# A decoder layer on one core: the last attention's output projection and norm moved into the first middle stage, other steps moved up at the seams

## The reference

```python
x = _layernorm(x + retention(x))          # q, k, v, gate; 16 heads; group norm per head; gate * ret @ wo + bo
x = _layernorm(x + ssm(ctx, gate_by=x))   # conv of 4 taps, silu, selective scan of 16 states, y * silu(x)
x = _layernorm(x + moe(x))                # 8 experts as low-rank additions to one FFN of 896, top 2
# ssm, with dt = softplus(dt_proj(dt_lo)):
state = state * exp(dt * A) + (dt * u) * B ;  y = sum_n state * C + D * u
# moe, for each of the two chosen experts e with routing weight rw:
x1 = x @ W1.T + lora1_e(x);  x3 = x @ W3.T + lora3_e(x);  h = silu(x1) * x3
out += (h @ W2.T + lora2_e(h)) * rw
```

## Time and profile before

| | |
|---|---|
| runs (us) | 480.14, 480.17, 482.71; median 480.17 |
| the profiled execution: its time, its span | 480.21, 478.5 |
| TensorE busy, VectorE, ScalarE, GpSimd | 391.9 (82%), 301.8 (63%), 189.8 (40%), 191.3 (40%) |
| mean granted TensorE clock | 0.913 of 2.4 GHz |

### The profile page before, as it was taken

How to read it: one execution, slowest core, us unless ns; L and a number is a source line. 1 busy time by engine, 2 the same in 40 slices (tenths; PEclk the granted TensorE clock), 3 DMA queues, 4 the chain that set the end, 5 groups by cost and what they waited for, 6 DMA issues and landing times.

```text
span 478.5 us, 7162 instructions
## 1 busy us (share of the span) xinstructions
PE 391.9 (82%) x2552; PEld 335.2 (70%) x2552; DVE 301.8 (63%) x643; ACT 189.8 (40%) x462; POOL 191.3 (40%) x207
## 2 busy tenths in 40 slices
PE   3776986878778557989798788979977899999993
PEld 2454765667556446889587778958776898789992
DVE  5546465675884619999236899942779993382224
ACT  3681557444424614453423635432264532131010
POOL 6015455246320454772214677131377632141221
PEclk9957899989859568999979899997989999999999
DMA  7640270000002101230300133020003300000000
GB/s 223 230 179 18 78 242 1 23 22 2 13 24 88 40 6 44 90 121 0 92 0 24 44 111 103 10 90 2 22 34 115 96 23 0 0 2 23 1 1 22
DMA packets 12339, 27.03 MB, mean 56 GB/s; under 512 B 1800, under 2 KB 3088, under 8 KB 12048
## 3 DMA queue, kind: packets, MB, share of 16 engines
q1 hardware_dynamic: 11440, 25.00, 15.8%
q10 hardware_dynamic: 864, 1.57, 1.0%
HBM read 25.39 MB, written 1.18 MB: 56 GB/s over the span
## 4 chain that ended last, share of the span: by engine, by line
PE 42%; DVE 30%; issue 14%; ACT 5%; POOL 5%; DMA 1%; SPq 1%; DVEq 0%; POOLq 0%; ACTq 0%
PE gen L1051 12%; PE xf L1051 11%; PE a2p L1051 9%; DVE ret L1597 6%; PE ret L1051 6%; DVE gen L1597 6%; DVE fth L1858 3%; PE acc L1051 3%; DVE ring L1605 2%; DVE sc L1614 2%; DVE ring L1671 2%; DVE cv L1537 2%; DMA wattn_sb<-in_wattn 1%; PE xf L1130 1%; POOL rs L598 1%
## 5 line engine op out<-in xcount | busy, mean ns | idle before, releaser
L1051 PE MATMUL xf<-am,wsplit 128*128 128x256 f32 x672 | 97.3, 296 | 0.1
L1051 PEld LDWEIGHTS xf<-am,wsplit 128*128 128x128 f32 x672 | 88.3, 197 | 2.2 <-DVE work L1869 0.5
L567 POOL TENSOR_TENSOR ring<-decay,brow 128x512 f32<-128x512 f32 x48 | 62.1, 1307 | 21.4 <-PE acc L1051 20.3
L672 POOL TENSOR_TENSOR work<-work,ratioT 128x256 f32<-128x256 f32 x28 | 20.6, 737 | 110.7 <-DVE work L1869 110.5
L1858 DVE SCALAR_TENSOR_TENSOR fth<-fth,xf 128x256 f32<-128x256 f32 x56 | 23.3, 415 | 62.2 <-ACT fth L998 62.1
L1051 PE MATMUL a2p<-work,wff_sb 128*128 128x256 f32 x224 | 60.1, 392 | 0.5 <-POOL work L672 0.5
L998 ACT ACTIVATE fth<-xf 128x256 f32<-128x256 f32 x56 | 20.9, 374 | 83.7 <-PE xf L1051 78.4
L1051 PE MATMUL xf<-x2s,wsplit 128*128 128x256 f32 x336 | 51.2, 303 | 0.4
L1051 PE MATMUL acc<-ident,ring 128*128 128x128 f32 x256 | 38.9, 281 | 12.8 <-DVE ring L1605 12.5
L1051 PEld LDWEIGHTS xf<-x2s,wsplit 128*128 128x128 f32 x336 | 45.4, 198 | 2.1 <-DVE work L1869 1.1
L1051 PEld LDWEIGHTS acc<-ident,ring 128*128 128x128 f32 x256 | 31.1, 145 | 18.6 <-DVE ring L1605 14.9
(11 more groups left out here) (278 smaller groups left out, 752.9 us busy)
## 6 DMA issues: line engine op xcount, KB each, us to landing
brow<-bc_dram SPq DMA_DIRECT2D x24, 256.0 KB, 3.6
crow<-bc_dram SPq DMA_DIRECT2D x24, 256.0 KB, 3.2
work<-in_wsp SPq DMA_DIRECT2D x3, 896.0 KB, 9.1
wff_sb<-in_wff SPq DMA_DIRECT2D x2, 896.0 KB, 7.7
am<-bc_dram SPq DMA_DIRECT2D x1, 1536.0 KB, 7.7
wattn_sb<-in_wattn SPq DMA_DIRECT2D x1, 1280.0 KB, 5.7
xT_sb<-in_xT SPq DMA_DIRECT2D x4, 256.0 KB, 2.7
wff_sb<-in_wff SPq DMA_DIRECT2D x3, 256.0 KB, 4.8
```

The source lines that it names most:

```text
L567: pool.tensor_tensor(ring[:, i % RING], du_of(b)[:, j].unsqueeze(1).broadcast_to([P, UN, S]), brow[:, c % 2], ALU.mult).then_inc(sem["driv ...
L672: pool.tensor_tensor(xs[:, n % 4], fq[:, m % 2], ratioT[:], ALU.mult).then_inc(sem["xs_ready"], 1)
L1051: return pe.matmul(o, l, r, skip_group_check=True, **kw)
```

## The change

The slots of `first` go from 21 to 18. The last attention's projection is in n = 2 of the first middle stage, its add and statistics in n = 3, root, shift and apply in n = 4. In `first`, GpSimd's `inputs` and two drives go from slot 16 to 15, `bias(3)` to 17, `start_y` on ScalarE from slot 17 to 16; GpSimd's `mk1` add goes behind the two lows. The finished batch's norm is applied by ScalarE (`finished`), behind a shift by VectorE (`norm_shift` for `norm_apply`), and ScalarE issues all stores.

In the stages: on TensorE `start_y` goes from n = 0 to 1, `base(12)` ahead of `flip_x2`, `low_rank` behind `logits`, `down` 2 and 3 to n = 12, 4 to n = 13, 5 behind it; A1 comes in n = 12; `route_rows` and `step_size` come ahead of `shrink(12)`, MK and MD ahead of `shrink(13)` and A3 behind MD. On VectorE the conv's first two steps go from n = 9 to the start of n = 11, the other four to its end, `conv_gate` from n = 10 to the start of n = 13, between the two parts of `route`, `second_part` to the start of n = 12. On ScalarE `normed`, `turned` and `rounded` are at the end of n = 11, `conv_tanh`, `weighed` and `low_rank` in n = 12, `routed`, softplus and its logarithm after n = 13 and ahead of `spread`, `start_y` ahead of the second pair of `am_high`, the decays behind it. DBL and DT are in bank 1.

```diff
...
-    a2_ready=3, down_done=1, r3_ready=8, r3_pow=1, y_ready=2,
+    a2_ready=3, down_done=1, r3_ready=8, r3_pow=1, y_shift=1, y_ready=2,
 )
...
 -SLOTS = 21
+SLOTS = 18
...
 ROTATED = gen_order()
-STAGED = []
+STAGED = [("OUT", B - 1)]
 for _b in range(1, B):
     _n = [_b + 1] if _b + 1 < B else []
-    STAGED += [("Z", _b)] + [("IN", n) for n in _n] + [("DBL", n) for n in _n] + [("X2", _b)] + [("DT", n) for n in _n]
-    STAGED += [(name, _b) for name in ("LG", "A1", "A3", "RT", "MK", "MD", "RW")]
+    STAGED += [("Z", _b)] + [("IN", n) for n in _n] + [("X2", _b), ("LG", _b)] + [("DBL", n) for n in _n] + [("A1", _b), ("RT", _b)]
+    STAGED += [("DT", n) for n in _n] + [(name, _b) for name in ("MK", "MD", "A3", "RW")]
...
-OWN_BANK = {("X2", 0): 4, ("A1", 0): 5, ("A3", 0): 2, ("VAR", B - 1): 0, ("RW", 0): 0, ("OUT", B - 1): 0}
+OWN_BANK = {("X2", 0): 4, ("A1", 0): 5, ("A3", 0): 2, ("VAR", B - 1): 0, ("RW", 0): 0}
...
-GEN_AT += [{"X2": 1, "A1": 5, "A3": 1}.get(name, 0) for name, _ in STAGED]
+GEN_AT += [{"X2": 1, "DBL": 1, "DT": 1, "A1": 5, "A3": 1}.get(name, 0) for name, _ in STAGED]
...
-DOWNS = {10: (0, 1), 11: (2,), 12: (3, 4), 13: (5,)}
+DOWNS = {10: (0, 1), 12: (2, 3)}
...
-            def store(fb):
-                need(sp, "y_ready", fb, 2)
-                sp.dma_start(of(out, fb), yo[:]).then_inc(sem["y_out"], 16)
...
                 spread(b)
-            store(B - 1)
             need(sp, "y_out", B, 0)
...
                 mkT = mkTs[b % 2]
-                pool.tensor_tensor(mkT[:, 1], mkT[:, 0], mkT[:, 1], ALU.add).then_inc(sem["mk1_ready"], 1)
                 for i in (2, 3):
...
                                        ).then_inc(sem["aml_pool"], 1)
+                pool.tensor_tensor(mkT[:, 1], mkT[:, 0], mkT[:, 1], ALU.add).then_inc(sem["mk1_ready"], 1)
...
                         root(b, ve, rs, "r2_ready", 9, "r2_pow")
-                    if i == 16:
+                    if i == 15:
                         inputs(nb)
...
                         drive_unit(nb, 1)
+                    if i == 16:
+                        second_masks(b)
+                    if i == 17:
                         bias(B - 1)
-                        second_masks(b)
...
                         root(fb - 1, ve3, rs3, "r3_ready", 8, "r3_pow")
+                    if n == 4 and fb == 0:
+                        root(B - 1, ve1, rs1, "r1_ready", 7, "r1_pow")
                     if b is not None:
...
                         decays(nb, 0)
+                        start_y(nb)
                     if i == 17:
-                        start_y(nb)
                         decays(nb, 1)
...
+            def finished(fb):
+                need(act, "y_shift", fb, 1)
+                for t in range(NT):
+                    act.activation(yo[:, t], r3[:, t], ACT.Identity, bias=nm3[:, t:t + 1], scale=rs3[:, t:t + 1]
+                                   ).then_inc(sem["y_ready"], 1)
+                need(act, "y_ready", fb, 2)
+                act.dma_start(of(out, fb), yo[:]).then_inc(sem["y_out"], 16)
             def stage(b, fb, nb):
                 for n in range(len(MAIN)):
-                    if b is not None and n == 11:
-                        normed(b)
                     need(act, "xf_filled", fb, n + 1)
...
                     if n == 2 and fb > 0:
-                        need(act, "y_ready", fb - 1, 2)
-                        act.dma_start(of(out, fb - 1), yo[:]).then_inc(sem["y_out"], 16)
+                        finished(fb - 1)
+                    if n == 4 and fb == 0:
+                        attended(B - 1)
                     if n == 4:
...
                         act.activation(keep[:], x2[:], ACT.Copy).then_inc(sem["keep_ready"], 1)
-                    if nb is not None:
-                        if n == 8:
-                            conv_input(nb)
-                        if n == 10:
-                            conv_tanh(nb)
-                        if n == 11:
-                            low_rank(nb)
-                    if b is not None and n == 12:
+                    if nb is not None and n == 8:
+                        conv_input(nb)
+                    if b is not None and n == 11:
+                        normed(b)
                         turned(b)
...
                     if nb is not None and n == 12:
-                        softplus_exp(nb)
-                    if b is not None and n == 13:
+                        conv_tanh(nb)
+                    if b is not None and n == 12:
                         weighed(b)
+                    if nb is not None and n == 12:
+                        low_rank(nb)
+                if b is not None:
+                    routed(b)
                 if nb is not None:
+                    softplus_exp(nb)
                     softplus_log(nb)
                 if b is not None:
-                    routed(b)
                     spread(b)
...
                 if nb is not None:
-                    decays(nb, 0)
+                    start_y(nb)
                 if b is not None:
...
                 if nb is not None:
-                    start_y(nb)
+                    decays(nb, 0)
                     decays(nb, 1)
...
                     ratios(b)
+                if b is None:
+                    finished(fb)
...
                         shrink(fb, n - LAG)
-                    hidden(fb, n, n <= 1)
+                    hidden(fb, n, n <= 1 or n == 12 and b is not None)
+                    if n == len(MAIN) - 1 and b is not None:
+                        route_rows(b)
+                        if nb is not None:
+                            step_size(nb)
+                        down(fb, 4)
                     if n >= LAG:
...
                     if b is not None:
-                        if n == 0:
+                        if n == 1:
                             start_y(b, fb)
...
                             add_states(b, i)
+                        if n == 2 and fb == 0:
+                            attention_out(B - 1)
                         if n == 4:
                             token_z(b)
-                    if nb is not None:
-                        if n == 7:
-                            context(nb)
-                        if n == 11:
-                            low_rank(nb)
+                    if nb is not None and n == 7:
+                        context(nb)
                     if b is not None and n == 11:
+                        base(fb, 12)
                         flip_x2(b)
-                    if nb is not None and n == 12:
-                        step_size(nb)
                     if b is not None and n == 12:
                         logits(b)
+                        if nb is not None:
+                            low_rank(nb)
                     for m in sums.get(n, ()):
                         down(fb, m)
-                    if b is not None and n == 13:
+                    if b is not None and n == 12:
                         expert_inputs(b, "A1", A1)
-                        expert_inputs(b, "A3", A3)
                 if b is not None:
-                    route_rows(b)
+                    spread_rows(b, "MK", 0)
+                    down(fb, 5)
+                    spread_rows(b, "MD", 1)
+                    expert_inputs(b, "A3", A3)
                 shrink(fb, len(MAIN) - 1)
...
                     base(b, 1)
-                    spread_rows(b, "MK", 0)
-                    spread_rows(b, "MD", 1)
                 down(fb, FM - 1)
...
-            def conv(b):
+            def conv(b, i0=0, i1=2 * DC - 2):
...
                         i = 2 * k + j
+                        if not i0 <= i < i1:
+                            continue
                         if i >= 2:
...
                 dve.scalar_tensor_tensor(nm_[:], mv_[:, :, 0], -1.0, rs_[:], ALU.mult, ALU.mult).then_inc(sem[done], 1)
-            def norm_apply(b, src, mv_, rs_, dst, pow_, done):
-                need(dve, pow_, b, 1)
-                for t in range(NT):
-                    dve.tensor_scalar(dst[:, t], src[:, t], mv_[:, t, 0:1], rs_[:, t:t + 1], ALU.subtract, ALU.mult
-                                      ).then_inc(sem[done], 1)
...
                     units = SCANS[n] if b is not None else []
+                    if nb is not None and n == 11:
+                        conv(nb, 0, 2)
                     if b is not None and n == 11:
                         norm_shift(b, mv, rs, nm, "r2_pow", "r2_shift")
+                    if b is not None and n == 12:
+                        second_part(b)
+                    if b is not None and n == 13:
+                        route(b, 0)
+                        if nb is not None:
+                            conv_gate(nb)
+                        route(b, 1)
                     for i in units[:1]:
...
                     if n == 2 and fb > 0:
-                        norm_apply(fb - 1, r3, mv3, rs3, yo, "r3_pow", "y_ready")
```

(22 more changed lines are left out.)

## The result

The changed kernel takes 457.12 us (median of 4 runs, 456.57 to 457.71) against 480.15 us of the kernel before in the same comparison: ratio 0.9509, 95% interval 0.9474 to 0.9545. The forecast was 455.0, its own range 450 to 460. The profiled execution took 456.57 us with a span of 454.8, 23.7 us less than before, at a mean clock of 0.928 (0.913 before).

A forecast was written before the change was run, and what follows sets the result against it. VectorE was taken to bound the scan stretches and TensorE the seams, with a 9.05 us hole ending `first`. Terms 9.0 + 2.0 - 0.5 + 12.0 + 2.5 = 25.0 us gave 455.0 us, range 450 to 460.

The forecast's parts named there:

- first hole: End of `first`, where TensorE idles 9.05 us waiting for `gated(3)`: moving the last attention gains 9.0 us net.
- seams one and two: Passages between stages with a next batch: reordered products and banks gain 6.0 us each, 12.0 us.
- norm: Finished batch's norm leaves VectorE in the scan stretch of two stages: 1.0 us each, 2.0 us gained.
- seam three: The seam with no next batch: only the `base(12)`, `shrink(11)` and `down` moves, 2.5 us gained.
- tail: End of the kernel, where nothing covers the norm's shift and ScalarE's apply: 0.5 us lost.
- signs set for being right: Timeline marks: first tanh near 169.6, second stage's scan 1 14 to 17 us earlier, 2 to 3 us gap before MD.
- signs of being wrong: Seam stretch at clock 0.50 over 4 us, VectorE idle over 2 us among scans, first stage's start waiting for GpSimd.
- TensorE's balance: Seam lower bound of 1.8 us: 4.3 us idle and 1.95 us lost to the clock before, 4.4 us idle after.
- The seams give nothing: Rival, chance 0.17: seams one and two's new waits and a clock fall after each take all their gain, 467.2 us.
- The first hole does not close: Rival, chance 0.05: a late bank or buffer release leaves scan 1 gaining 3 us instead of 12.2, 464.2 us.
- Slower: Rival, chance 0.05: TensorE stays at 1.2 GHz from `low_rank`'s wait to next stage's n = 2, both seams, 493 us.
- Everything fits: Rival, chance 0.12: no clock fall, 7.9 us gained at two seams and 3.5 at the third, 450.4 us.

The follow-up runs named there:

- e1: The kernel before with only the last attention's move (slots 21 to 18, its steps into n = 2 to 4): 470.61 us, ratio 0.9792.
- e4: The changed kernel with GpSimd's `inputs` and two drives of `first` back in slot 16: 455.98 us, ratio 0.9499.
- e9: The changed kernel with `inputs` and drives of `first` back in slot 16 and `low_rank` behind `down` 2 and 3: 451.15 us, ratio 0.9372.
- e3: The changed kernel with the finished batch's norm applied by VectorE again, as before the change: 461.15 us, ratio 0.9587.
- e6: The changed kernel with `low_rank` behind `down` 2 and 3 in n = 12 instead of ahead of them: 454.68 us, ratio 0.9441.
- e8: The changed kernel with the edits of e4, e6 and e7 together: 452.28 us, ratio 0.9388.
- e2: The changed kernel without the last attention's move (21 slots again), so seams, norm and slot moves only: 463.87 us, ratio 0.9658.
- e10: e8 plus a wait: at a seam GpSimd's two drives start only when VectorE has written both lows: 448.46 us, ratio 0.9311.
- e7: The changed kernel with MK copied ahead of the softplus logarithm and mask slot 0 ahead of `step_sum`: 459.07 us, ratio 0.9514.
- e5: The changed kernel unaltered, run again for comparison on one chip: 457.97 us, ratio 0.9518.

## Why the prediction was right, and which term was off

The measured span is 23.7 us shorter for a forecast of 25.0. The parts are further off than the sum, and partly cancel: first hole 2.3 us too much, seams one and two 1.6 too little, norm and seam three 0.4 too much each, tail 0.2 too little. Three of the signs set for being right did not come: the first tanh is at 172.74 (169.6), scan 1 of the second stage 13.5 us earlier (14 to 17), the gap before MD 1.19 us (2 to 3). The others did. Of the signs of being wrong, a start that waits for GpSimd came in a hidden form: ScalarE waits for VectorE, which GpSimd's drives had held up.

**First hole** (taken 9.0 us: 12.2 at the first tanh less 3.2; measured 6.7: 9.0 at the first tanh and 9.4 at scan 1, less 2.7 from there to the last scan). This is the mis-sized term. The mechanism holds: no wait for `gated(3)`, the attention's steps between the scans (add at 187.41, between scans 5 and 6), 0.84 us lost behind the apply at n = 4 for a forecast of 1.0. The step that failed is that GpSimd's `inputs` and drives in slot 15 were costed by their own durations (2.50 us) alone, as a move on GpSimd's queue. Beside VectorE's lows they took 3.34, the lows 2.36 instead of 1.29, the shift 1.21 instead of 0.15, and so VectorE's `gvar` and the last two masked products behind it came 2.1 us late.

ScalarE's `am_high` waits for these products: at 164.77, after 4.24 us idle, where it stood at 161.63 after 2.10 us before. Everything of ScalarE up to the first tanh is queued behind it, the decay of scan 0 too; `norm_lin`, at 170.53, waits for nothing of its own. The forecast said of ScalarE's inputs that they hold; this one did not.

e1, e4 and e9 show it: with the drives in slot 16, e9's lows start at 160.01, as the changed kernel's at 159.97, and its scan 0 at 167.73 instead of 169.83. The forecast had the drives end near 161.5; they end at 163.45. The remaining 1 us of the tanh is where this execution stood already when the last part of `first` began: a product of the router's rows that both profiles have is at 151.42, 150.41 before, and 150.3 to 153.0 over the experiments. What makes this part differ is not shown.

The long shift of 1.21 us had a row and was made a bound, for the moved shifts. There it proved rightly short (0.15 and 0.16 us). Whether GpSimd's drives would lengthen the large lows as well, which the moved drives now met, was not asked, nor whether they would lengthen L1916 in the seams.

**The norm** (2.0): 0.8 us in each of two stages, 1.6. The apply of 1.08 us is covered by the scans, as argued; e3 gives 1.9 for it. **The tail** (-0.5): -0.3.

**Seams one and two** (6.0 each): 6.8 each. The forecast lay between 7.9 without and 5.5 with a fall of the clock. In the profiled execution the clock did not fall, so the working's own value was 7.9, and the gain was 1.1 short of it. The last masked input ends at 248.37, 5.9 us earlier beyond the first hole's 6.7, for a forecast of 7.0; some 0.75 of the missing 1.1 us are L1916's (1.44 us for 0.69), between `shrink(13)` and the lows on that path.

The clock was misread. The forecast counted 3.9 us at a granted clock of 0.50 before the change and 1.95 us lost. That was the length of the stretch chosen; the rows beside it have 0.96 and 0.95, and the clock was at 0.50 from 238.3 to 245.1, for 6.8 us, which costs 3.4. TensorE's balance then gives a lower bound of 3.3 us a seam, not 1.8. More than half of the seam's gain up to scan 0 (3.4 of 5.4 us) is that the fall did not come back. That was not to be known from the rows of before, and not every execution has it: e4's seam two lost 3.9 us to it. That the seams did better than 6.0 is in this part luck.

Wait by wait: `low_rank` was forecast at 1.8 us and took 1.92, and e6 shows its price by removing it. MD was forecast at 2.6 and took 1.19. The copy of MK came when it was expected (239.85, with the first hole's 6.7 us 246.6, for 246.3 to 246.9); TensorE reached MD 1.8 us later than expected (239.29, so 246.0 for 244.2), since the products before it took longer. Removing that gap is worth nothing while the lows then meet the drives (e8 against e9). **Seam three** (2.5): 2.1.

**The rivals.** "The seams give nothing" (467.2) is refuted by e2, which gains 16.8 us without the first hole, in a profile without a fall; its condition, a fall after each wait, was met in e4's seam two, which comes near it. "The first hole does not close" is refuted by e1. "Slower" (the clock stays at half) did not happen in any profile; the longest stretch at 0.50 in a seam was 6.8 us (238.3 to 245.1 before the change, 303.4 to 310.2 in e4). "Everything fits" (450.4) did not happen in the changed kernel; e10, which is another kernel, passes that time at 448.5, with the collisions and both waits of TensorE out.

**The table load.** ScalarE's load in front of ln took 1.28 us. It began 0.02 us behind the activation before it (vpad, to 238.00), ln began 0.01 us behind the load, and MK's copy at 239.85, as ln ended. So the load cost this chain its own 1.28 us and no more, which is what the forecast had counted.

## What to carry to other kernels

When an instruction is moved, look not only at its own queue but at what the neighbouring engine runs at the new time: VectorE instructions with both inputs in SBUF and GpSimd's products, like the lows and drives of this kernel (lows 3.46 us beside the drives in e8, 1.28 apart in e10), are to be kept apart, and one wait that orders them can be cheaper than the overlap (2.15 us a seam, e8 to e10). A wait that is removed shows its worth only if what is late next is not made later by it (e8 against e9). Before a clock fall is counted, its ends are to be found: a window that lies inside it shows a part of it. Two variants that differ by less than a clock fall costs should be compared by timelines too, since an execution with a fall hides 3 us (e4), and what a removed wait seems to give can be a fall that did not come.

## What the runs showed of the hardware

**VectorE and GpSimd side by side.** In e8's seam the two drives begin at 240.44 and the lows end at 244.29:

```profile
240.44 3.30 POOL L561 TENSOR_TENSOR ring<-decay,brow 128x512 f32<-128x512 f32 x2
240.83 3.46 DVE L1655 TENSOR_TENSOR am<-dmask,am 128x512 fp32r<-128x512 f32 x2
```

Together they take 3.85 us; apart they take 2.51 + 1.28 = 3.79. Overlap gained nothing, and VectorE paid more of it (2.18 us longer, the drives 0.79). Taken one by one, they end in turn: the first drive at 242.06, the first low at 242.61, the second drive at 243.74, the second low at 244.29. So each low takes 1.77 us here (0.68 alone) and ends some 0.55 us after a drive, as it would if it had waited for that drive; the rows show the times, not the cause. The other cases of this study: two lows 2.36 us beside two drives of 3.34, and the 128x2 shift behind them 1.21 us for 0.15 (end of the changed kernel's `first`), and L1916 1.44 us for 0.69 beside a drive (its seam one). All of these read both inputs from SBUF. The masked products of e10, with one input in PSUM, took 0.68 us beside the drives, and the two drives took 2.51 us.

**The clock** fell to 0.50 behind a TensorE gap of 1.92 us in some seams and not in others of the same order. Of the twelve such gaps in the profiles it fell behind five: both of e4 and of e7, one of e3, none in the changed kernel, e2 and e5. Where that gap is closed and the one of 1.19 us before MD is left (e6, e9), it fell behind one of four. In the four seams with neither gap (e8, e10) it did not fall up to scan 0; behind e8's second one it did, at 0.50 from 328.4 to 331.2, after an idle time of 2.10 us of TensorE that ended at 327.09. So closing the larger gap alone does not rule a fall out; that closing both does so for the seam is likely, from four cases. The four runs each of e6, e8, e9 and e10 lie within 1.7 us of one another, while e4's span 4.6.
